# Half of the next group's up products in the attention phase, the last tile's codes and down product behind the phase border

## What is computed

```python
x = x + tanh(g_xattn[0]) * L0_xattn(layernorm(x), ctx, W, b)
#   ex = ix @ W.T + b; softmax(ex @ (ctx @ W.T + b).T) @ ctx
x = x + tanh(g_ffn[0]) * L0_ffn(layernorm(x), w_up, w_down)
#   ternary_linear(gelu(ternary_linear(x, w_up)), w_down), each input divided by its RMS
x = x + tanh(g_xattn[1]) * L1_xattn(layernorm(x), ctx, mask, Wq, bq, Wkv, bkv, Wout, bout, 16)
#   16 heads of 32: softmax(q k.T / sqrt(32), masked) v, then @ Wout + bout
x = x + tanh(g_ffn[1]) * L1_ffn(layernorm(x), gate_w, up_w, down_w, s_in, s_in_down)
#   nvfp4_linear(silu(gate) * up, down_w): inputs and weights rounded to
#   FP4 codes (0, .5, 1, 1.5, 2, 3, 4, 6) with an FP8 scale for each block of 16
```

## Time and profile before

| | |
|---|---|
| median of 3 runs | 1785.82 us (1785.01 to 1788.02) |
| the profiled execution | 1785.0 us, its span 1782.9 us |
| mean granted TensorE clock | 0.908 |
| VectorE (DVE) busy | 1421.2 us, 80% of the span |
| TensorE (PE) busy | 1345.8 us, 75% |
| ScalarE (ACT) busy | 692.2 us, 39% |
| GpSimd (POOL) busy | 244.8 us, 14% |

### The profile page before, as it was taken

One profiled execution on the slowest core, in us unless ns is written; L12 is line 12 of the kernel. 1 busy time (PEld: TensorE's weight loads), 2 busy tenths in 40 slices (PEclk: granted clock), 3 DMA queues, 4 the chain that ended last, 5 costly groups with the idle time before them and its releaser, 6 DMA issues.

```text
span 1782.9 us, 22428 instructions
## 1 busy us (share of the span) xinstructions
PE 1345.8 (75%) x8120; PEld 693.2 (39%) x8120; DVE 1421.2 (80%) x2437; ACT 692.2 (39%) x2105; POOL 244.8 (14%) x197
## 2 busy tenths in 40 slices
PE   5044837799787978698878888797879886988663
PEld 4021314434453436344543345343634353444321
DVE  6989896877887697787787888778877878786696
ACT  2113206442464327342645156422743264425210
POOL 1102300131003200130013100310022001310000
PEclk9556868999899999999999999998999999999888
DMA  9165861041203320233004210322014100420011
GB/s 350 69 237 144 206 156 36 7 86 39 72 1 60 71 59 13 36 64 78 24 7 89 58 50 1 68 63 60 14 41 90 48 25 7 88 60 24 7 30 47
DMA packets 267395, 119.68 MB, mean 67 GB/s; under 512 B 244090, under 2 KB 244602, under 8 KB 265750
## 3 DMA queue, kind: packets, MB, share of 16 engines
q1 hardware_dynamic: 267286, 118.27, 26.8%
HBM read 49.04 MB, written 8.39 MB: 32 GB/s over the span
## 4 chain that ended last, share of the span: by engine, by line
DVE 46%; PE 32%; ACT 8%; issue 6%; DMA 4%; SPq 2%; POOL 0%; DVEq 0%; ACTq 0%
PE bank L1064 24%; PE bank L1151 6%; DVE amax L819 4%; ACT region L529 4%; DVE hid L824 3%; DVE pair L828 3%; DVE stats L680 2%; DVE th L861 2%; DMA hqt<-pair 2%; DVE region L912 2%; DVE region L711 2%; DVE pair L843 2%; DVE sr L794 2%; DVE hid L865 2%; DVE pair L836 1%
## 5 line engine op out<-in xcount | busy, mean ns | idle before, releaser
L1151 PE MATMUL bank<-w_dn,region 128*128 128x512 fp8e4 x1024 | 243.0, 385 | 36.9 <-DMA region<-region 36.9
L1064 PE MATMUL bank<-w_up,xt 128*128 128x512 fp8e4 x1024 | 245.8, 387 | 31.6 <-ACT region L493 17.0
L1064 PE MATMUL bank<-w_gate,xqt 128*128 128x512 bf16 x512 | 148.9, 418 | 125.4 <-DVE th L861 82.3
L502 ACT ACTIVATE th<-bank,half_cg 128x512 f32<-128x512 f32 x128 | 88.0, 688 | 346.7 <-PE bank L1064 346.7
L420 POOL TENSOR_TENSOR region<-g,region 128x512 f16<-128x512 f32 x128 | 180.4, 1414 | 296.8 <-ACT region L493 288.7
L861 DVE SCALAR_TENSOR_TENSOR th<-th,bank 128x512 f32<-128x512 f32 x128 | 87.7, 685 | 132.8 <-ACT th L502 132.8
L529 ACT ACTIVATE region<-bank,nm 128x77 f32<-128x77 f32 x512 | 161.7, 356 | 63.0 <-DVE nm L907 63.0
L490 ACT ACTIVATE g<-bank 128x512 f32<-128x512 f32 x128 | 76.4, 597 | 245.1 <-PE bank L1064 186.2
L1064 PE MATMUL bank<-w_down,hqt 128*128 128x512 bf16 x512 | 130.3, 413 | 53.4 <-DMA hqt<-pair 53.4
L1151 PEld LDWEIGHTS bank<-w_dn,region 128*128 128x128 f16 x1024 | 101.2, 99 | 162.3 <-DMA region<-region 38.4
L1064 PEld LDWEIGHTS bank<-w_up,xt 128*128 128x128 f16 x1024 | 101.2, 100 | 160.9 <-ACT region L493 20.9
(11 more groups left out here) (206 smaller groups left out, 2449.7 us busy)
## 6 DMA issues: line engine op xcount, KB each, us to landing
xin<-in_x SPq DMA_DIRECT2D x16, 512.0 KB, 4.5
out_x<-x SPq DMA_DIRECT2D x16, 512.0 KB, 2.7
region<-in_w_up_t SPq DMA_DIRECT2D x1, 4096.0 KB, 12.9
hid<-in_gate_w SPq DMA_DIRECT2D x4, 1024.0 KB, 5.4
x<-in_gate_w SPq DMA_DIRECT2D x4, 1024.0 KB, 6.7
hid<-in_up_w SPq DMA_DIRECT2D x4, 1024.0 KB, 5.2
x<-in_up_w SPq DMA_DIRECT2D x4, 1024.0 KB, 5.6
hid<-in_down_w SPq DMA_DIRECT2D x4, 1024.0 KB, 5.0
```

Of the source, the lines that this page charges most:

```text
L502: eng.activation(th[:, u % 2, :], bank[4][:, :], ACT.Tanh, scale=half_cg[:, :]).then_inc(sg["th"], 1)
L1064: last = mm(out, lhs, rhs, start=(n == 0), stop=(n == len(pairs) - 1))
L1151: last = mm(bank[2 + t % 2][:, :], ht[i][:, t % 2, f, :], w_dn[:, f, :], start=(f == 0 and i == 0), stop=(f == KF - 1 and i == 1))
```

## The change

Four things are moved, and nothing is computed in another way.

1. The front of the next group begins a step earlier (`START1`), its last transpositions stand together in step 17 (with banks 4 and 5 for tiles 2 and 3), and eight up products follow in steps 18 to 25, with their gelu, instead of three. Phase B has the other eight, and its table is shorter: gate and up pieces from slots 2, 8, 14 and 20, down quarters from slot 5, 29 slots instead of 33.
2. The last tile's hidden codes are in five parts: four in slots 24 to 27, the fifth in step 1 of the next phase A. Its down product stands at the head of step 4, into bank 3, and its output sum in step 6.
3. Normalisation 1 is made in halves: tiles 0 and 1 have their statistics in slot 24 and are normalised in slot 26; tiles 2 and 3 have statistics in steps 2 and 3 of phase A and are normalised in step 5. The first codes of x stand two steps earlier.
4. POOL makes `root4(1)` behind the seventh subtraction instead of ahead of the first. SP transposes the second half of the x codes behind the four transpositions of tiles 0 and 1.

The diff, cut to its core:

```diff
@@ -42,37 +42,44 @@
 QUANT_PARTS = 5
-START1 = (1, 2, 7, 8)
+START1 = (0, 1, 6, 7)
+STATS1_AT = {2: (2,), 3: (3,)}
+NORM1_AT = 5
+LATE_QUANT, LATE_DOWN, LATE_OUT = 1, 4, 6
...
 NORM2_AT = VAR2_AT + 2
-T2_AT = {NORM2_AT + 1: (0, 1), NORM2_AT + 2: (2, 3)}
-UP_AT = {NORM2_AT + 3: 0, NORM2_AT + 4: 1, NORM2_AT + 5: 2}
-VAR4_AT = TILES * NC + 3
+T2_AT = NORM2_AT + 1
+UPS_A = 8
+UP_AT = {T2_AT + 1 + i: i for i in range(UPS_A)}
+VAR4_AT = TILES * NC + 1
 X4_STEPS = {VAR4_AT + 2: (0, 1), VAR4_AT + 3: (2,), VAR4_AT + 4: (3,), VAR4_AT + 5: (4,)}
-STEPS = max(TILES * NC + 10, NORM2_AT + 6)
+STEPS = max(TILES * NC + 10, T2_AT + 1 + UPS_A)
...
 UP_SLOTS = TILES * CHUNKS
-SLOT_DOWN = 2 * CHUNKS
-SLOT_MS = {UP_SLOTS // 2 + 2: 0, UP_SLOTS + 2: 1}
+SLOT_DOWN = 5
+SLOT_MS, SLOT_RS = {2: 0, 10: 1}, {6: 0, 13: 1}
...
 SLOT_T3, SLOT_Q = SLOT_NORM3 + 1, SLOT_NORM3 + 2
-SLOT_NORM1 = SLOT_Q + 2
+SLOT_STATS1, SLOT_NORM1 = SLOT_Q, SLOT_Q + 2
 X4_AT = {1: (0, 1), 2: (2, 3), 3: (4,)}
-TILE_AT = (2, 9, 16, 23)
+TILE_AT = (2, 8, 14, 20)
 GU_AT = {TILE_AT[t] + n: 4 * t + n for t in range(TILES) for n in range(4)}
-QUANT_AT = {TILE_AT[t] + 4 + i: (t, q) for t in range(TILES) for i, q in enumerate(((0, 1, 2), (3, 4)))}
-POST_AT = {TILE_AT[t] + (10 if t < TILES - 1 else 7): t for t in range(TILES)}
-SLOTS = max([SLOT_Q + NC] + [s + 2 for s in POST_AT]) + 1
+QUANT_AT = {TILE_AT[t] + 4 + i: (t, q) for t in range(TILES - 1) for i, q in enumerate(((0, 1, 2), (3, 4)))}
+QUANT_AT.update({SLOT_Q + q: (TILES - 1, (q,)) for q in range(4)})
+DOWN4_AT = {TILE_AT[0] + 9: 0, TILE_AT[1] + 9: 1, SLOT_Q: 2}
+OUT4_AT = {TILE_AT[0] + 10: 0, TILE_AT[1] + 10: 1, SLOT_Q + NC: 2}
+SLOTS = SLOT_Q + NC + 1
 TAIL_PARTS = ((0, 1), (2,), (3,), (4,))
-PREP_SLOTS = SLOT_NORM3 + 3
+PREP_SLOTS = SLOT_STATS1
...
 PREP_AT = {s: PREPS[len(PREPS) * s // PREP_SLOTS:len(PREPS) * (s + 1) // PREP_SLOTS] for s in range(PREP_SLOTS)}
-POOL_MS = {UP_SLOTS // 2 + 2: 0, UP_SLOTS: 1}
+POOL_MS = {UPS_A + 1: 0, UP_SLOTS: 1}
+ROOT4_AFTER = UPS_A - 2
@@ -343,11 +354,11 @@
             def turns(g, g1, g2):
-                for h in range(2):
-                    turn_x(g, h)
+                turn_x(g, 0)
...
                     turn_ht(g1, 1)
+                turn_x(g, 1)
@@ -395,6 +404,12 @@
                 eng.tensor_tensor(rstd[:, 0, :], ve[:, 0, :], powers[:, 0, :], ALU.pow).then_inc(sg[f"rstd{stage}"], 1)
+            def root1(g, a):
+                want(pool, "var1", g, a + 1)
+                ts = slice(2 * a, 2 * a + 2)
+                eng.tensor_tensor(rstd[:, 0, ts], ve[:, 0, ts], powers[:, 0, ts], ALU.pow).then_inc(sg["rstd1"], 1)
@@ -403,14 +418,13 @@
                 if g1 is not None:
+                    root1(g1, 1)
...
                     root4(g3, 0)
-            def phase_b(g, s4, g1):
-                if s4 is not None:
-                    root4(s4, 1)
+            def phase_b(g, s4):
@@ -419,26 +433,26 @@
                                       ALU.subtract).then_inc(sg["hl"], 1)
+                    if s4 is not None and s == ROOT4_AFTER:
+                        root4(s4, 1)
...
                 root(3, g)
-                if g1 is not None:
-                    root(1, g1)
-            root(1, 0)
+                if g + 1 < GROUPS:
+                    root1(g + 1, 0)
+            root1(0, 0)
...
@@ -479,8 +493,9 @@
                     eng.activation(pt1[0][:, u % 2, :], bank[u % 2][0:M, P:2 * P], ACT.Copy).then_inc(sg["p1h"], 1)
-                for t in T2_AT.get(n - 1, ()):
-                    x_hi(2, g, t)
+                if n == T2_AT + 1:
+                    for t in range(TILES):
+                        x_hi(2, g, t)
@@ -543,11 +558,13 @@
                         attend(g3, n)
+                    if g1 is not None and n in UP_AT:
+                        up(g1, UP_AT[n])
...
                 for s in range(SLOTS):
-                    if s < UP_SLOTS:
-                        up(g, s)
+                    if s < UP_SLOTS - UPS_A:
+                        up(g, s + UPS_A)
@@ -692,9 +707,9 @@
                 eng.tensor_scalar(dst, mv[:, s, ts, 1], LN_EPS, None, ALU.add).then_inc(sg[f"var{stage}"], 1)
-            def norm(stage, g, src):
-                want(dve, f"rstd{stage}", g)
+            def norm(stage, g, src, tiles=range(TILES)):
+                want(dve, f"rstd{stage}", g, 1 + tiles[0] // 2 if stage == 1 else None)
@@ -873,9 +896,9 @@
                 quantise(buf[:, :], h_sc[:, :], h_g[:, :], parts, sg["hq"])
-            def out4(g, t):
+            def out4(g, t, b=7):
                 want(dve, "dn4", g, t + 1)
-                eng.scalar_tensor_tensor(x3[:, t, :], bank[7][:, :], kd[:, :], x3[:, t, :], ALU.mult,
+                eng.scalar_tensor_tensor(x3[:, t, :], bank[b][:, :], kd[:, :], x3[:, t, :], ALU.mult,
@@ -941,17 +964,21 @@
                         attend(g3, n)
+                    if g3 and n == LATE_QUANT:
+                        quant4(g3 - 1, TILES - 1, (4,))
+                    if g3 and n == LATE_OUT:
+                        out4(g3 - 1, TILES - 1, 3)
...
                         stage1(g1, n)
-            def phase_b(g, s4, g1):
+            def phase_b(g, s4):
...
                         mean_square(g, SLOT_MS[s])
-                    if s - 1 in SLOT_MS:
-                        root_scale(g, SLOT_MS[s - 1])
+                    if s in SLOT_RS:
+                        root_scale(g, SLOT_RS[s])
@@ -969,8 +996,11 @@
                                           ALU.subtract).then_inc(sg["ql"], 1)
-                    if s == SLOT_NORM1 and g1 is not None:
-                        norm1(g1)
+                    if g + 1 < GROUPS:
+                        if s == SLOT_STATS1:
+                            stats1(g + 1)
+                        if s == SLOT_NORM1:
+                            norm(1, g + 1, xin, (0, 1))
@@ -984,8 +1014,8 @@
                             quant4(s4, t, q)
-                        if s - 2 in POST_AT:
-                            out4(s4, POST_AT[s - 2])
+                        if s in OUT4_AT:
+                            out4(s4, OUT4_AT[s])
@@ -1091,14 +1120,17 @@
                 want(pe, f"xn{stage}", g, t + 1)
-                if t >= 2:
+                if t >= 2 and stage == 2:
+                    if g:
+                        want(pe, "p3", g - 1)
+                elif t >= 2:
...
                 for k in range(KD):
-                    last = tr(bank[t % 2][:, k * P:(k + 1) * P], xn[:, t, k * P:(k + 1) * P], ident[:, :])
+                    last = tr(state_bank(stage, t)[:, k * P:(k + 1) * P], xn[:, t, k * P:(k + 1) * P], ident[:, :])
@@ -1123,17 +1155,20 @@
                     x_t(1, g, u)
-                for t in T2_AT.get(n, ()):
-                    x_t(2, g, t)
+                if n == T2_AT:
+                    for t in range(TILES):
+                        x_t(2, g, t)
...
                 if s < 2:
-                    want(pe, "xl2", g)
+                    want(pe, "xl2", g, s + 1)
...
                     want(pe, "hh", g, s - 1)
+                    if n == 0 and t >= 2:
+                        want(pe, "xl2", g, t + 1)
@@ -1163,13 +1198,18 @@
                         want(pe, "p3", g)
+                        if g + 1 < GROUPS:
+                            want(pe, "xl2", g + 1)
...
                     last.then_inc(sg["gate" if i == 0 else "gu"], 1)
-            def down4(g, t):
-                want(pe, *(("out4", g, t) if t else ("p3l", g)))
+            def down4(g, t, b=7):
+                if b == 7:
+                    want(pe, *(("out4", g, t) if t else ("p3l", g)))
+                else:
+                    want(pe, "qh", g + 1)
                 want(pe, "hqt", g, 16 * (t + 1))
-                product(bank[7][:, :], [(hqt[:, k, :], w_down[:, k, :]) for k in range(KF)]).then_inc(sg["dn4"], 1)
+                product(bank[b][:, :], [(hqt[:, k, :], w_down[:, k, :]) for k in range(KF)]).then_inc(sg["dn4"], 1)
@@ -1188,10 +1228,10 @@
                     b = t // 2
-                    if n == 0:
-                        want(pe, "ql", g)
+                    if t == 0:
+                        want(pe, "ql", g, c + 1)
+                    if n == 0 and g:
+                        want(pe, "hid", g - 1)
@@ -1218,6 +1258,8 @@
                         want(pe, "p3l", g, m - 1)
+                    elif m == 1 and g:
+                        want(pe, "out4", g - 1, TILES - 1)
@@ -1226,6 +1268,8 @@
                         want(pe, "x3", g, t)
+                    elif g:
+                        want(pe, "out4", g - 1)
@@ -1240,6 +1284,8 @@
                 for n in range(STEPS):
+                    if g3 and n == LATE_DOWN:
+                        down4(g3 - 1, TILES - 1, 3)
@@ -1247,8 +1293,8 @@
                 for s in range(SLOTS):
-                    if s < UP_SLOTS and s not in UP_AT.values():
-                        up(g, s)
+                    if s < UP_SLOTS - UPS_A:
+                        up(g, s + UPS_A)
```

66 lines of the change are left out of this document (33 added, 33 removed).

## The result

The changed kernel takes **1802.19 us** (median of 5 runs, 1801.46 to 1818.91), the kernel before 1786.2 (median of 5, 1785.01 to 1788.02). The ratio is 1.0104, with a 95% interval of 1.008 to 1.0127. It is 16 us slower, where 1775 was forecast. The time lies inside the range, but on the other side of no change.

What follows compares the result with a forecast made beforehand. VectorE and TensorE, neither full, wait for each other by turns. VectorE's terms sum to +0.5 us a group, +3.5 over seven; with −8, −2.9 and −3 at the ends, 1785.0 becomes 1774.6, forecast 1775 us, range 1742 to 1806.

Steps and rivals of the forecast that it cites:

- the two waits of VectorE: Per group, about 5 us for the power of tiles 2 and 3, and about 4 for step 4's score product.
- the idles of 3 to 4.5 behind the codes: TensorE in phase B: idles of 3.5 to 4.5 us forecast behind each tile's codes.
- mask and scale steps of the x codes: Small VectorE operations on x codes: if they take 1.2 us throughout, the forecast is wrong and the time 1801.
- the waits for tanh: VectorE waiting for ScalarE's tanh in phase B: about 14 us a group forecast, 18.3 before.
- Term 7: The rest, per group: second aggregation and variance step +0.5 us, query's low half +1.0, TensorE's clock +1.0 (bounds 0, +2.5).
- Term 4: Waits for tanh in phase B: −4.1 us a group, leaving 14.2; bounds −6 and 0.
- Term 5: End of phase A: wait of 5.0 us for POOL's power, output sums' waits 2.3; +3.3 a group, bounds 0 and 5.
- Terms 1 to 3: End of B −2.3 us, start of A −3.8, last down product inside A +3.8, per group.
- Term 6: VectorE's codes colliding with POOL's subtractions: 7.0 us a group against 5.9, so +1.1; bounds −2 and +4.8.
- the rival that had POOL in the way: End of A and start of B: every subtraction in x codes costs its full 0.96 us; 1801 us, chance 0.23.
- Term 8: The ends: prologue −8 us (bounds 0 and −14), last phase B −2.9 more, tail −3.
- The rival of the filled gaps: Power ready when A's last sum comes, step 4 late anyway: 3.6 us a group more gained, 1750 us, chance 0.25.

Runs made afterwards that it cites:

- e1: The changed kernel with ten unread matmuls ahead of each of hidden pieces 1, 5, 9 and 13: 1777.31 us, ratio 0.9955.
- e3: The changed kernel with four up products in phase A instead of eight and POOL's power behind the third subtraction: 1822.03 us, ratio 1.02.
- e2: The changed kernel with POOL's power for tiles 2 and 3 behind its fifth subtraction instead of its seventh: 1778.96 us, ratio 0.9959.
- e5: e2 with the last part of the last tile's codes, its down product and output sum back at the end of phase B: 1825.2 us, ratio 1.0208.
- e0: The changed kernel measured again, nothing edited: 1801.82 us, ratio 1.0106.
- e9: e2 with the prologue's load of x ahead of the last weight piece in SP's order: 1775.95 us, ratio 0.9949.
- e6: The kernel before with unread matmuls ahead of hidden pieces 0, 1 and 13 and the last down product: 1791.73 us, ratio 1.0027.
- e11: The changed kernel with the edits of e1, e2 and e9, and the late down product in step 6, its sum in step 8: 1753.15 us, ratio 0.982.

## Why the prediction was wrong

It forecast 0.5 us a group more and 14 less at the ends. In the groups compared above it is 6.3 more (4.2 in the next, at a higher clock), and by the medians the whole kernel is 16 more where 11 less was forecast. Of the signs that it named, the two waits of VectorE came (4.5 and 2.9), the idles of 3 to 4.5 behind the codes too, and of the ten mask and scale steps of the x codes nine took 0.20 to 0.23 and one 1.06. What did not come is the waits for tanh, 20.4 for about 14.

- **Term 7, the clock, is the step that failed.** It was put at +1.0 with 2.5 as its upper bound, as half of one slow stretch. e1 prices it: with the same order and the clock held in phase B, the waits for tanh are 14.1 instead of 20.4 in the groups of the profiled executions, and the kernel is 25 us shorter by the medians, 3.6 a group. At 1777.3 it is then 9 us faster than the kernel before, close to the 11 that were forecast. What the prediction had seen was the place: it named the idles of 3.5 to 5 ahead of pieces 1, 5, 9 and 13. It counted only the longer matmuls, and took over from before that a slow stretch mostly lies under other work. In the thinned-out phase B VectorE stands waiting for just those pieces. The other item of the term that a row shows, +1.0 for the query's low half, came as said (1.1).
- **Term 4, the waits for tanh: right as a sum, as far as the order goes** (14.2 said, 14.1 in e1, for 18.3), but its parts were not, so the agreement is partly luck. The second tile was to lose 5.1 and lost 2.8 (6.5 to 3.7), the third 0.6 and lost 2.4 (6.2 to 3.8), the first was to gain 1.7 and gained 1.0. e3 against e2 confirms the direction from the other side.
- **Term 5, POOL's power behind the seventh subtraction: right in size, wrong in reach.** 5.0 was said, 4.5 measured, 2.3 for the output products said and measured. But it was booked as a wait that ends where it ends. e2 shows that it goes on: TensorE idles, falls to 1.2 GHz, and the first tile's waits for tanh are 2.6 longer. e1, which leaves the power's wait and holds the clock, takes off the same 2.6.
- **Terms 1 to 3, the border.** The two small waits at B's end are gone as said. The wait of step 4 was put at 3.8 and is 2.9, the waits of the first steps of A fell from 4.3 to 3.8, and the sum of the three, −2.3, came out at −2.9. The reading is good; the undoing in e5 was misjudged, for there the cover was gone as well.
- **Term 6, collisions, and the second aggregation: +1.6 said, −0.4 measured** (VectorE busy 153.2 for 153.6). POOL stood waiting for gelu passes and for the power's input while VectorE coded, so the two met less. The time came out beside that of the rival that had POOL in the way (1801), but by another mechanism; e2, where the power is early, has some of it (busy 156.8).
- **Not priced at all**: the output product of the first layer's attention, moved a step earlier with `START1`, makes VectorE wait 2.3 to 2.8 in every kernel with the change, where the earlier trace rows have 2.0 for a score product nearby. The reductions of the steps before it wait 2.9 in the group read and 1.3 in the next, for about 1 before.
- **Term 8, the ends.** The prologue was put at −8 and gained nothing: the first phase A began at 289.4 instead of 288.8 (286.8 in e0). A new wait of 5.9 for POOL's RMS power came in, and x was 7.7 late instead of gone, since SP issues its load behind a weight piece (e9). The tail gave 3.6 for 3 said. The last group came out 0.8 longer where the others are 3.8 to 7.3 longer, so it gave somewhat more than the 2.9 said.

The rival of the filled gaps has a slip in its sum: a group that gains 4.1 on the forecast makes 1775 − 29 = 1746, not 1750. Nothing hangs on it. The chances were set too low on the slow side mainly for one reason: the slower rival was built on collisions, and the clock, which was seen, was given a bound from its own length and not from who waits behind it.

## What to carry to other kernels

A product that is late because its engine has just idled costs its waiter the idle, the slow stretch behind it, and whatever the waiter then frees late. When work is moved out of a phase, look at the engine that loses it: price the clock by who waits for the first products after each new gap, and try a few matmuls on constant data in those gaps before giving the move up. Look then at which product is slow: in e1 they kept the clock through the products that VectorE waits for, in e6 they kept it at a product that nobody waited for and a slow stretch came at the next one.

A small operation on a third engine (0.7 us of POOL here) belongs in its queue where its input is ready, and its place by itself was worth 23 us in the changed kernel.

## What was not expected of the hardware

Idle stretches of TensorE of the same length, in the same place of two groups, were followed by 1.2 GHz in one and by 2.4 GHz in the other. In the kernel before, piece 13 stands behind an idle of 3.79 both times:

```profile
829.88 1.89 PE L1064 MATMUL bank<-w_gate,xqt 128*128 128x512 bf16 x4 [3.79 <-DVE th L861]
...
1021.22 1.04 PE L1064 MATMUL bank<-w_gate,xqt 128*128 128x512 bf16 x4 [3.79 <-DVE th L861]
```

And the clock need not be low at the first matmul behind the idle: at 990.78 of the changed kernel it fell while the second product ran. In the group of the changed kernel shown above all four idles, of 2.98 to 4.53, were followed by 1.2 GHz.

The profiled execution of the changed kernel was the longest of its series both times (1818.9 and 1816.7 against 1800 to 1806), at a mean clock of 0.886 and 0.885 against 0.891 or more in the first series. Why it is bound to that execution no run tells; the profiled executions of e1, e9 and e11 were not the long ones of their series.
